# Expert scores alone in 32-row groups, two lanes issued together: a two-layer decoder on one core

## The reference

```python
qkv = x @ iw.T + ib
q, k, v = jnp.split(qkv, 3, axis=-1)               # 16 heads of 16 features
scores = jnp.einsum('bhqd,bhkd->bhqk', q, k) / scale
attn = jax.nn.softmax(scores, axis=-1)
o = jnp.einsum('bhqk,bhkd->bhqd', attn, v)         # heads joined again
x = _layernorm(x + o @ ow.T + ob, n1w, n1b)
ff = jax.nn.relu(x @ l1w.T + l1b) @ l2w.T + l2b
return _layernorm(x + ff, n2w, n2b)
```

## Time and profile before

| | |
|---|---|
| median of 3 runs | 3447.11 us (3442.37 to 3447.35) |
| span of the profiled execution | 3440.4 us |
| PE busy | 3307.1 us, 96% of the span |
| DVE busy | 2123.6 us, 62% |
| ACT busy | 1940.5 us, 56% |
| POOL busy | 378.0 us, 11% |
| third pass | from about 2356 us to the end |

### The profile page before, as it was taken

One profiled execution on the slowest core, in us unless ns is written; L12 is line 12 of the kernel. 1 busy time (PEld: TensorE's weight loads), 2 busy tenths in 40 slices (PEclk: granted clock), 3 DMA queues, 4 the chain that ended last, 5 costly groups with the idle time before them and its releaser, 6 DMA issues. The chain is left out here.

```text
span 3440.4 us, 79739 instructions
## 1 busy us (share of the span) xinstructions
PE 3307.1 (96%) x30487; PEld 2486.5 (72%) x30487; DVE 2123.6 (62%) x6895; ACT 1940.5 (56%) x6527; POOL 378.0 (11%) x457
## 2 busy tenths in 40 slices
PE   7999999999799999999999999997999999999998
PEld 5777777777666666666666666665888888888887
DVE  4666666666355555555545455554777767777776
ACT  2666566655444444454444545444767667767775
POOL 1112111211000000000000000000111111111111
PEclk9999999999899999999999999997999999999999
DMA  3000000000201010100000000005010022021000
GB/s 118 13 14 15 16 13 14 15 16 16 64 1 30 11 30 11 30 11 23 18 18 22 18 22 18 17 2 200 15 18 15 15 60 60 15 60 18 15 15 11
DMA packets 63957, 95.58 MB, mean 28 GB/s; under 512 B 7218, under 2 KB 59010, under 8 KB 62034
## 3 DMA queue, kind: packets, MB, share of 16 engines
q1 hardware_dynamic: 55202, 82.74, 7.9%
q0 software_dynamic: 8368, 7.70, 1.9%
HBM read 72.04 MB, written 18.37 MB: 26 GB/s over the span
## 5 line engine op out<-in xcount | busy, mean ns | idle before, releaser
L1422 DVE CUSTOM_DVE_ANT_0 PON<-pps,PMR 112x375 f32<-112x375 f32 x512 | 260.0, 545 | 265.0 <-PE pps L1168 264.4
L1656 PE MATMUL bps<-BXT,Bwexp 128*128 128x112 f32 x3072 | 373.3, 279 | 9.1 <-DMA Bwexp<-in_we 3.5
L1656 PEld LDWEIGHTS bps<-BXT,Bwexp 128*128 128x128 f32 x3072 | 362.3, 194 | 26.4 <-ACT BXT L1781 14.6
L1764 ACT ACTIVATE BPT<-bps,Blow 112x112 f32<-112x112 f32 x1024 | 349.1, 392 | 20.5 <-DVE Blow L1881 20.0
L1301 ACT ACTIVATE PPT<-pps,mcol 125x896 f32<-125x896 f32 x192 | 193.3, 1007 | 201.5 <-PE pps L1187 201.1
L1764 ACT ACTIVATION_READ_ACCUMULATOR BPT<-bps,Blow 112x1 f32 x1024 | 250.0, 246 | 0.0
L1729 PE MATMUL bps<-Bwexp,BPT 128*112 128x256 f32 x1024 | 235.4, 381 | 0.0
L892 POOL TENSOR_TENSOR rstd<-var,nhalf 112x1 f32<-112x1 f32 (+1 forms) x96 | 149.5, 1557 | 709.9 <-DVE var L810 470.1
L1168 PE MATMUL pps<-PKT,PQM 64*112 64x375 f32 x1024 | 222.2, 513 | 3.7 <-DVE Pmx L1422 1.7
L708 ACT ACTIVATE PT<-PT,low 112x112 f32<-112x112 f32 x512 | 191.8, 386 | 37.6 <-DVE low L867 37.6
L1456 POOL TENSOR_TENSOR Prstd<-Pvar,nhalf 112x1 f32<-112x1 f32 x128 | 72.0, 565 | 1281.2 <-DVE Pvar L1336 1281.2
(11 more groups left out here) (308 smaller groups left out, 7297.9 us busy)
## 6 DMA issues: line engine op xcount, KB each, us to landing
Bwexp<-in_we SPq DMA_DIRECT2D x7, 2311.0 KB, 22.5
PCX<-in_ctx SPq DMA_DIRECT2D x24, 375.0 KB
out<-BY POOLq DMA_DIRECT2D x64, 112.0 KB, 3.0
BXIN<-xmid SPq DMA_DIRECT2D x61, 112.0 KB, 2.0
Bwexp<-in_we SPq DMA_DIRECT2D x7, 770.0 KB, 5.1
Brexp<-in_re SPq DMA_DIRECT2D x7, 672.0 KB, 9.5
XIN<-in_x SPq DMA_DIRECT2D x32, 112.0 KB
CX<-in_ctx SPq DMA_DIRECT2D x32, 112.0 KB
```

The source lines that it names most:

```text
L1422: m = v.tensor_tensor_reduce(out=ON[s][0:T, i * LC:(i + 1) * LC], in0=bank[s][i][0:T, 0:LC], in1=MR[s][:, :], scale=1.0, scalar=-3.0e38, o ...
L1656: m = mm(o[:, j * T:(j + 1) * T], wt[:, c, n0 + j * 128:n0 + (j + 1) * 128], rhs[:, c, :], start=(c == 0), stop=(c == 1))
L1764: m = A(PT[s][0:T, h, :], bank[s][i][0:T, v * T:(v + 1) * T], ACT.Exp, scale=0.25, bias=low[s][:, h:h + 1], accum_out=sums[s][:, h:h + 1])
```

## The change

1. In the scores of the third pass each of the four groups of 32 rows works alone. A group holds two heads of each half of the features, so two masked copies of the queries are enough (`QM` has 2 and not 4, the mask `hm2` is made once from `hm4` in the first pass's preparation).
2. Lanes 0 and 1, and lanes 2 and 3, are pairs. The step of both is issued in the piece of the even lane; the odd lane's piece is empty. At a step the even lane uses rows 0 to 63 and the odd lane 64 to 127, at the next step the other way round (`half`). Ahead of it TensorE waits for both lanes. PV reads the heads from their new places.
3. `run_slots` and its place numbers are replaced by `run_order`, with strings that give the lane of each piece. The strings of the first and second pass give the old order; those of the third are new.
4. The wait of Y for earlier additions to the output asks for the lane's own last one and not for all four of the round before.

```diff
+def run_order(eng, order, batch, count, extra=None):
+    runs = {4: extra} if extra else {}
+    begun = {s: 0 for s in LANES}
+    for mark in order:
+        s = int(mark)
...
+        if s not in runs:
+            runs[s], begun[s] = batch(s, begun[s]), begun[s] + 1
+        if next(runs[s], "over") == "over":
+            runs.pop(s)
...
+        hm2 = sb("hm2", [128, 2, T])[:, :, :]
...
+        rows = [slice(32 * j, 32 * j + 32) for j in range(4)]
+
+        def half(s, step):
+
+            return step if s % 2 == 0 else 1 - step
...
+                v.tensor_tensor(hm2, hm4[:, 0:2, :], hm4[:, 2:4, :], ALU.add)
...
-            QM = lanes("QM", [128, C2, 4, T])
+            QM = lanes("QM", [128, C2, 2, T])
...
-                    for c in range(C2):
-                        yield
-                        if c == 0:
-                            t.wait(masked_ready[s], 2)
-                            t.wait(vx_read[s])
-                        else:
-                            t.wait(exp_ready[s])
-                        for v in range(4):
-                            for i in range(2):
-                                m = mm(bank[s][i][0:T, v * T:(v + 1) * T], QM[s][side[i], c, v, :], KT[s][side[i], c, :], start=True, stop=True)
-                        m.then_inc(s_psum[s], 1)
+                    for step in range(2):
+                        yield
+                        if s % 2 == 0:
+                            for k in (s, s + 1):
+                                if step == 0:
+                                    tallies[k].wait(masked_ready[k], 2)
+                                    tallies[k].wait(vx_read[k])
+                                else:
+                                    tallies[k].wait(exp_ready[k])
+                            for n in range(4):
+                                for k in (s, s + 1):
+                                    for i in range(2):
+                                        g = rows[2 * half(k, step) + i]
+                                        m = mm(bank[k][i][0:T, n * T:(n + 1) * T], QM[k][g, n // 2, n % 2, :], KT[k][g, n // 2, :], start=True, stop=True)
+                                    if n == 3:
+                                        m.then_inc(s_psum[k], 1)
...
-                                       PT[s][0:T, 8 * c + 2 * k + n, :], start=(c == 0 and n == 0), stop=(n == 1), skip_group_check=True)
+                                       PT[s][0:T, 8 * half(s, k // 2) + 4 * (k % 2) + 2 * c + n, :], start=(c == 0 and n == 0), stop=(n == 1), skip_group_check=True)
...
-                        v.scalar_tensor_tensor(out=QM[s][:, c, :, :], in0=b1[:, c * T:(c + 1) * T].unsqueeze(1).to_broadcast((128, 4, T)),
-                                               scalar=wc(s, "bq")[:, c:c + 1], in1=hm4[:, :, :],
+                        v.scalar_tensor_tensor(out=QM[s][:, c, :, :], in0=b1[:, c * T:(c + 1) * T].unsqueeze(1).to_broadcast((128, 2, T)),
+                                               scalar=wc(s, "bq")[:, c:c + 1], in1=hm2,
...
-                    dve.wait_ge(added, at.n[s] * 64 + 16)
+                    if rd:
+                        dve.wait_ge(added, rd * 64 + (16 - 16 * s))
+                    else:
+                        dve.wait_ge(added, 16)
```

More of the change, by code:

```diff
@@ L262, in skip @@
         self.seen[sem.num] = self.seen.get(sem.num, 0) + n
-class Place:
-    def __init__(self, n, last=False):
-        self.n, self.last, self.first = n, last, False
-def run_slots(eng, lanes, count, batch, turns, lead, first, last, aside=None):
-    at, runs = Place([0] * len(lanes)), [None] * len(lanes)
-    before = [sum(1 for x in turns[s] if x < lead[s]) for s in lanes]
-    def begin(s):
-        runs[s] = [batch(s, at), 0]
-    def work(s, places, turn, end):
-        while runs[s][1] < end and places[runs[s][1]] <= turn:
-            next(runs[s][0], None)
-            runs[s][1] += 1
-    def middle(i):
-        at.n = [i] * len(lanes)
-        for turn in range(SPAN):
-            for s in lanes:
-                local = (turn + lead[s]) % SPAN
-                if local == 0:
-                    at.n = [i + 1 if k == s and lead[s] else at.n[k] for k in lanes]
-                    begin(s)
-                work(s, turns[s], local, len(turns[s]))
-    for s in lanes:
-        if lead[s]:
-            begin(s)
-    at.first = True
-    others = aside(at) if aside else iter(())
-    for turn in range(SPAN):
-        for s in lanes:
-            if lead[s]:
-                work(s, first[s], turn, before[s])
-        if turn >= 400 and turn % 20 == 0:
-            next(others, None)
-    for _ in others:
-        pass
-    at.first = False
-    for i in range(count - 1):
-        middle(i)
-    at.n, at.last = [count - 1] * len(lanes), True
-    for s in lanes:
-        if not lead[s]:
-            begin(s)
-    for turn in range(SPAN):
-        for s in lanes:
-            work(s, last[s], turn, len(turns[s]))
+def run_order(eng, order, batch, count, extra=None):
[3 more added lines that the diff above has]
+        s = int(mark)
+        if s == 4:
+            next(runs[4], None)
+            continue
+        if s not in runs:
+            runs[s], begun[s] = batch(s, begun[s]), begun[s] + 1
+        if next(runs[s], "over") == "over":
+            runs.pop(s)
+    assert all(n == count for n in begun.values()) and set(runs) <= {4}
+    for _ in runs.get(4, ()):
+        raise AssertionError("pieces left over")
 def span_of(sems):
@@ L449, in _, with batch @@
                 sp.dma_start(mrow, mneg[:, :]).then_inc(mask_stored, 16)
-                def batch(s, at):
+                def batch(s, rd):
                     t = Tally(sp)
                     yield
-                    more = not at.last
+                    more = rd != quarter - 1
                     if more:
                         t.wait(var_ready[s], 3)
-                        sp.dma_start(XIN[s][:, :], x[bass.ds(at.n[s] + (s * quarter + 1), 1), :, :].rearrange("a t d -> (a t) d")).then_inc(x_in[s], 16)
-                        sp.dma_start(CX[s][:, :], ctx[bass.ds(at.n[s] + (s * quarter + 1), 1), 0:T, :].rearrange("a t d -> (a t) d")).then_inc(x_in[s], 16)
+                        sp.dma_start(XIN[s][:, :], x[bass.ds(rd + (s * quarter + 1), 1), :, :].rearrange("a t d -> (a t) d")).then_inc(x_in[s], 16)
+                        sp.dma_start(CX[s][:, :], ctx[bass.ds(rd + (s * quarter + 1), 1), 0:T, :].rearrange("a t d -> (a t) d")).then_inc(x_in[s], 16)
                     else:
@@ L549, in batch @@
                     t.wait(tp_ready[s])
-                    if at.first:
+                    if rd == 0:
                         pe.wait_ge(weights_in, 16)
@@ L751, in step, with keep @@
                     t.wait(chain)
-                def keep(at):
+                def keep():
                     step(v.tensor_reduce(msum[:, 0:16], ident.rearrange("p (i r) -> p r i", i=2)[:, 0:16, :], AX_X, ALU.add))
@@ L875, in batch @@
                     v.tensor_tensor(X[s][:, :], X[s][:, :], b1[0:T, 0:D], ALU.add).then_inc(xn_ready[s], 1)
-                run_slots(dve, LANES, quarter, batch, TURNS["dve1"], TURNS["lead1"], FIRST["dve1"], LAST["dve1"], aside=keep)
+                run_order(dve, ORDER["dve1"], batch, quarter, extra=keep())
                 for s in LANES:
@@ L900, in batch @@
                     inverse_root(1)
-                run_slots(pool, LANES, quarter, batch, TURNS["pool1"], TURNS["lead1"], FIRST["pool1"], LAST["pool1"])
+                run_order(pool, ORDER["pool1"], batch, quarter)
                 for s in LANES:
@@ L961, in build @@
             yo = W("yo", C2)
-            rows = [slice(32 * j, 32 * j + 32) for j in range(4)]
             first_loaded, row_loaded = cast_ready, bias_ready
@@ L982, in _, with batch @@
                 sp.dma_start(gbt[:, :], gb.to_broadcast((B, E))).then_inc(loaded, 16)
-                def batch(s, at):
+                def batch(s, rd):
                     t = Tally(sp)
-                    sp.dma_start(MR[s][:, :], mrow[bass.ds(at.n[s] + s * quarter, 1), :].to_broadcast((T, LC))).then_inc(m_in[s], 16)
+                    sp.dma_start(MR[s][:, :], mrow[bass.ds(rd + s * quarter, 1), :].to_broadcast((T, LC))).then_inc(m_in[s], 16)
                     yield
-                    more = not at.last
+                    more = rd != quarter - 1
                     if more:
@@ L1440, in batch @@
                     normalise(X)
-                run_slots(dve, LANES, quarter, batch, TURNS["dve2"], TURNS["lead2"], FIRST["dve2"], LAST["dve2"])
+                run_order(dve, ORDER["dve2"], batch, quarter)
                 for s in LANES:
@@ L1469, in batch @@
                     inverse_root()
-                run_slots(pool, LANES, quarter, batch, TURNS["pool2"], TURNS["lead2"], FIRST["pool2"], LAST["pool2"])
+                run_order(pool, ORDER["pool2"], batch, quarter)
                 for s in LANES:
@@ L1601, in _, with batch @@
```

(13 more changed lines are left out.)

194 lines of the change are left out of this document (139 added, 55 removed), and 180 rows, old and new, of tables (FIRST, LAST, TURNS).

## The result

The changed kernel takes 3458.83 us (median of 5 runs, 3456.01 to 3467.35), the kernel before 3445.23 beside it (5 runs, 3442.37 to 3447.35): the medians differ by 13.6 us, and the ratio estimated from all runs is 1.0046, with an interval of 1.0033 to 1.0059. The forecast was 3434 and faster; the time is inside the range, the sign is wrong. The profiled executions have spans of 3440.4 and 3454.3 us; each is the fastest of its five runs.

The account below looks back on a forecast made before the run. TensorE was taken to bound the steady third pass, at work 98.6 of 100 us. Head +13.9, 14 rounds at -1.6 and tail -4.35 gave -12.8 us, from 3447.1 to 3434 us; range 3397 to 3465.

Parts of the forecast that it names:

- part 1: Third pass scores: one step for two lanes takes 0.97 us, 3.9 us less TensorE work a round.
- part 2: Query masking on VectorE: two copies save 0.5 us a batch, off TensorE's path.
- part 3: New third-pass order with paired lanes: waits take back part of the gain, round 63.6 us, 1.6 less than 65.19.
- The named waits: TensorE's waits in one new steady round, ahead of score steps, transpositions and other pieces: 4.1 us in sum.
- 0.2 for T's slower starts: Steady round on TensorE: transpositions start slower after other shapes, 0.2 us a round added to the waits.
- The head: Third pass start, lane 3's first X to its second: 67 us, 13.9 us longer than before.
- I keep it: Three exchanges of expert weights: their 0.77 us a round over the 65.19 us steady round stays as before.
- 0X: TensorE's wait before lane 0's X, for the go SyncE sends after lane 1's load: 0.65 us a round.
- D: Rival: the coupled softmax, VectorE's maxima queued behind other lanes' work, becomes the bound; rounds 65.4, 3460 us; chance 0.21.
- B: Rival: the new round's waits are hidden, no more than the old 2.0 us; round 61.3, 3402 us; chance 0.20.
- C: Rival: four row groups overlap only partly, score step 1.1 to 1.3 us, 3442 to 3455 us; chance 0.12.
- E: Rival: row groups don't overlap across lanes, score step 1.94 us, 3496 us; chance 0.05.

Follow-up runs that it names:

- two more edits to the order: Changed kernel, bias row early, plus lane 2's second maximum moved up and, from round three, SyncE's input and early weight loads ahead of starts and rows: 3430.26 us.
- its bias row early: Kernel before, with the bias row that VectorE's first sum reads loaded with the early expert weights: 3436.51 us, ratio 0.9970.

## Why the prediction was wrong

- **The step, part 1: right.** 0.98 us for four row groups, taken as 0.97. The Trainium skill's "TensorE: Matmul & The Clock Gate", Measured speedup vs the span model, gives 3.07 for four row tiles at 512 columns; at the 112 columns here four groups at a time lose nothing against two, 32 records take as long as 16 did. The measurement decides for this shape.
- **The mask, part 2: right.** Small groups and two copies alone leave the round at 65.15.
- **The round, part 3: nearly right.** 63.80 for 63.6. The named waits came to 3.24 us for 4.1 walked; but "0.2 for T's slower starts" should have been 1.2 to 1.3 (63.80 - 59.3 - 3.24). The old round had it in sight: 2.0 of waits and slower starts, of which only 0.49 had a name. 14 x 0.2 = 3 us.
- **The head: right as far as it was walked, ended too early.** 67.9 for 67, lane 3's second X 67.9 after the first. The walk had half clock only at the first projections; in the profile the granted clock fell back to 0.51 from 2390 to 2410, where score steps took 1.85 us, so that the number fits is partly luck. And lanes 1 and 0 were not at their steady distance by then, and their second batches took 85.1 and 73.6 us; lane 3 paid 5.9 us in its next two rounds. "14 rounds" of steady length was the wrong term behind that head.
- **"I keep it": the step that failed.** The 0.77 a round of the exchanges was carried over as a constant. It is no constant but a distance: rows that stand right behind the late weights land about 12 us after these go out, and what VectorE waits is 12 less the time at which XQ would have come anyway. The change moves SyncE's pieces too; its new order puts each lane's load_late and load_rows side by side, and XQ comes 2.3 to 5.2 us behind the late issue where it would have come 4.0 to 12.3 behind it before. The prediction walked SyncE's queue for one wait only (0X) and looked no further in it. 10.3 us: with the 5.9 of the start, the 3 of the round and 1.8 of head and tail this makes up the 21 us between -12.8 as forecast and +8.0 as traced (+13.9 less the 5.9 of run to run). The medians say the same more strongly: without exchanges the changed kernel is 3.4 us faster (3433.85 against 3437.24), too little to be told apart, and not 12.8, and the exchanges add 16. This step alone would leave a gain of 2.5 us by the profiles (12.8 less 10.3) and a loss of 3 by the medians; the other terms did the rest.
- **The rivals.** D's time, 3460, is near, and its sign is right, but by luck and not by its mechanism: the rounds are 63.8, not 65.4. B, C and E have their own answers above. That another part of the moved queue would get dearer was no rival at all.
- **The median and the profile.** The 6.7 us between span and median were taken as what lies outside of the span. The profiled execution took 3442.37, so only 2.0 lie outside; the other 4.7 are from run to run, as the first X is.

What stays open: why the clock rises late in some heads of the new order and the head varies from 67 to 73 us with it, and where a median execution of the changed kernel loses the 5 us more than the profiled one.

## What to carry to other kernels

When an order is written anew, walk every queue through the rare rounds too, with the bytes that stand ahead of each load: a load that is needed at once must not be issued behind a larger one that is needed late. A cost that shows up in a few rounds is best written as "landing time less what covers it", and taken again for the new order. A gain of 2 % on the bound engine's round was real here and was all given back at the ends and in three rounds; freed of the exchanges, and with two more edits to the order, the changed kernel came out 6 us ahead of the old one with its bias row early, which does not have those two edits.

## What was not expected of the hardware

Two loads on SyncE's queue moved 316 GB/s together, and the second stood behind the first: 672 KB issued 2 to 3.5 us behind 2311 KB landed 8 to 10 us after issue, and 5.1 us (median) after it when issued ahead. And 16 fp32 matmuls of 32 rows by 112 columns took 0.98 us when four row groups alternated and 1.47 when only two did, with nothing else changed than the order of issue.
